# Who issues the first loads: the two context transfers move from SyncE's queue to ScalarE's, ahead of its table load

## The reference, cut to what matters

```python
def _L0_xattn_ref(q, latent_kv, Wq, Wkv_expand, Wout):
    qp = q @ Wq.T
    kv = latent_kv @ Wkv_expand.T          # context (.., 256) -> keys and values, 1024 each
    k, v = jnp.split(kv, 2, axis=-1)
    ...
    scores = jnp.einsum('bhqd,bhkd->bhqk', qh, kh) * inv_sqrt_d
    scores = jnp.where(causal, scores, jnp.finfo(scores.dtype).min)
    attn = jax.nn.softmax(scores, axis=-1)
    out = jnp.einsum('bhqk,bhkd->bhqd', attn, vh)
    return out @ Wout.T

x = x + _L0_xattn_ref(_layernorm(x, axis=-1), ctx_512, Wq, Wkv_expand, Wout)
x = x + _L0_attn_ref(_layernorm(x, axis=-1), ...)   # gated MLP with quantized weights
x = x + _L0_ffn_ref(_layernorm(x, axis=-1), ...)    # 8 routed experts and a shared one
```

## Time and profile before

| | us |
|---|---|
| median of 3 runs | 627.8 (627.37 to 627.97) |
| the profiled execution | 628.29 |
| its span, first to last instruction | 626.5 |
| PE busy | 609.5 (97% of the span) |
| DVE busy | 507.5 (81%) |
| ACT busy | 427.5 (68%) |
| POOL busy | 192.8 (31%) |
| bytes moved | 177.91 MB, mean 284 GB/s |

### The profile page before, as it was taken

One profiled execution on the slowest core, in us unless ns is written; L12 is line 12 of the kernel. 1 busy time (PEld: TensorE's weight loads), 2 busy tenths in 40 slices (PEclk: granted clock), 3 DMA queues, 4 the chain that ended last, 5 costly groups with the idle time before them and its releaser, 6 DMA issues.

```text
span 626.5 us, 10607 instructions
## 1 busy us (share of the span) xinstructions
PE 609.5 (97%) x3624; PEld 477.4 (76%) x3625; DVE 507.5 (81%) x883; ACT 427.5 (68%) x563; POOL 192.8 (31%) x174
## 2 busy tenths in 40 slices
PE   7999999998999999999999999999999999999995
PEld 6778888887887444444567888898998989889784
DVE  5888888888787787889899479788696887968687
ACT  3998888889755988888585366649385583846630
POOL 2254445425100243435940310040330404314051
PEclk9999999999999999999999999999999999999999
DMA  8977776865236997936999759695886968769357
GB/s 311 421 311 310 304 307 243 310 268 201 101 138 248 416 367 282 383 123 252 402 357 419 323 195 322 244 385 205 310 309 211 384 230 307 291 237 367 121 174 271
DMA packets 31070, 177.91 MB, mean 284 GB/s; under 512 B 4064, under 2 KB 4064, under 8 KB 14784
## 3 DMA queue, kind: packets, MB, share of 16 engines
q1 hardware_dynamic: 25536, 158.64, 66.0%
q0 software_dynamic: 5504, 18.88, 8.3%
HBM read 154.30 MB, written 23.20 MB: 283 GB/s over the span
## 4 chain that ended last, share of the span: by engine, by line
PE 69%; ACT 13%; DVE 7%; DMA 4%; issue 3%; POOL 2%; SPq 0%; DVEq 0%; POOLq 0%; ACTq 0%
PE BK L2215 11%; PE BK L307 9%; PE BK L1903 8%; PE BK L1946 6%; PE BK L2218 4%; ACT RA L1395 4%; ACT PR L1422 4%; PE BK L313 3%; PE BK L314 3%; PE BK L319 3%; PE BK L2185 3%; PE BK L2173 2%; PE BK L1848 2%; DVE WL L1038 2%; PE BK L2171 2%
## 5 line engine op out<-in xcount | busy, mean ns | idle before, releaser
L2215 PE MATMUL BK<-EX,WH 128*128 128x320 f32 x384 | 99.4, 343 | 0.0
L705 POOL TENSOR_TENSOR WL<-RC,WH 128x2048 fp32r<-128x2048 f32 x7 | 45.6, 6508 | 167.9 <-ACT WH L1603 167.9
L1038 DVE TENSOR_TENSOR WL<-RA,WH 128x2048 fp32r<-128x2048 f32 x40 | 89.3, 2288 | 9.2 <-ACT WH L1603 8.8
L2218 PE MATMUL BK<-EX,WL 128*128 128x160 f32 x336 | 79.3, 236 | 0.0
L1603 ACT ACTIVATE WH<-RA 128x2048 fp32r<-128x2048 f32 x40 | 73.7, 1908 | 0.8 <-PE BK L1946 0.8
L2215 PEld LDWEIGHTS BK<-EX,WH 128*128 128x128 f32 x384 | 69.2, 189 | 0.0
L2218 PEld LDWEIGHTS BK<-EX,WL 128*128 128x128 f32 x336 | 64.2, 191 | 0.0
L655 POOL TENSOR_TENSOR HB<-HB,ND (+2 forms) x26 | 28.6, 1120 | 100.5 <-DVE BH L922 99.8
L1712 ACT ACTIVATE HX<-SR 128x320 fp32r<-128x320 f32 x16 | 7.5, 472 | 57.0 <-DVE SR L1088 57.0
L1494 ACT ACTIVATE RA<-RA,RT 128x2048 int16<-128x2048 f32 x22 | 43.7, 1997 | 2.7 <-DVE RT L852 1.9
L1903 PE MATMUL BK<-TG,XQ 128*128 128x512 bf16 x192 | 42.4, 379 | 0.1
(11 more groups left out here) (336 smaller groups left out, 1660.9 us busy)
## 6 DMA issues: line engine op xcount, KB each, us to landing
RA<-wbit SPq DMA_DIRECT2D x54, 1024.0 KB, 6.4
RA<-wmoe SPq DMA_DIRECT2D x40, 1024.0 KB, 6.2
RC<-wmoe SPq DMA_DIRECT2D x20, 1024.0 KB, 7.8
rows<-ZERO POOLq DMA_DIRECT2D x40, 256.0 KB, 8.2
XG<-rows SPq DMA_DIRECT2D x10, 512.0 KB, 3.6
rows<-YS SPq DMA_DIRECT2D x9, 512.0 KB, 4.1
RA<-wqk SPq DMA_DIRECT2D x7, 640.0 KB, 8.1
RA<-wo SPq DMA_DIRECT2D x4, 1024.0 KB, 8.0
```

Of the source, the lines that this page charges most:

```text
L705: e.tensor_tensor(WL[2][:, at], RC[5][:, :], WH[2][:, at].bitcast(f32), ALU.subtract).then_inc(free_c[5], 1)
L1038: e.tensor_tensor(WL[m][:, q * RAW:q * RAW + RAW], RC[j][:, :], WH[m][:, q * RAW:q * RAW + RAW].bitcast(f32), ALU.subtract)\
L2215: mm = e.matmul(bank[GBK[f]][:, 0:2 * R], WH[m][:, at], EX[:, k, :, :].rearrange("p a b -> p (a b)"), start=k == 0, stop=k == KD - 1)
L2218: e.matmul(bank[GBK[f]][:, 0:R], WL[m][:, at], EX[:, k, 0, :], start=False, stop=False)
```

## The change

The two loads of the context leave SyncE's program and become the first two instructions of ScalarE's, ahead of its table load. They have the same source, target, size and semaphore as before. SyncE's program begins with the first weight block, and everything behind it stands in the same order as before. Nothing else is changed.

```diff
         @blk.sync
         def _(e):
-            e.dma_start(CTX[:, 0, :], ctxT[:, 0, :]).then_inc(s("ctx_in"), 16)
             e.dma_start(RA[0][:, 0:DM], wv[:, 0:DM]).then_inc(s("wv_in"), 16)
-            e.dma_start(CTX[:, 1, :], ctxT[:, 1, :]).then_inc(s("ctx_in2"), 16)
             for t in range(NT):
...
         @blk.scalar
         def _(e):
+            e.dma_start(CTX[:, 0, :], ctxT[:, 0, :]).then_inc(s("ctx_in"), 16)
+            e.dma_start(CTX[:, 1, :], ctxT[:, 1, :]).then_inc(s("ctx_in2"), 16)
             e.preload_act_table(ACT.Sqrt)
+
             def context_hi(m):
```

## The result

The changed kernel takes 628.89 us (median of 22 runs, 627.95 to 630.88) and the kernel before 627.77 (22 runs beside them, 627.00 to 628.86). The ratio is 1.0018, with a 95% interval of 1.0012 to 1.0025: slower by 1.1 us. Forecast were 627.6 and a range up to 628.6, so the prediction was wrong in its sign, and the time lies 0.3 us outside its range. The loss is within the 0.2% that the prediction took for the same, and it is clear of zero.

A forecast was written before the change was run, and what follows sets the result against it. TensorE was taken to set the opening's pace, the DMA engines being the second limit. Shortening two waits (0.17 us on TensorE, 0.16 on VectorE) was to start the exponentials 0.20 sooner: 627.8 - 0.20 = 627.6 us, range 627.0 to 628.6.

The forecast's parts named there:

- The bound of the kernel: Opening: TensorE sets the pace, the DMA engines are the second limit, busy all the time from 6 us on.
- SyncE's issues, d = 0.3: SyncE's queue: two issues fewer shift the whole stream of loads sooner by d, taken as 0.3 us, between -0.3 and 0.78.
- ScalarE's issues: Ahead of ScalarE's table load: two added issues of 0.45 us each, table load at 1.70, hidden in idle time, cost 0.
- Context 0 is issued at about 0.80 as before: no change beyond sharing (below): First context load, now on ScalarE's queue: issue time unchanged at about 0.80, no cost entered for its landing.
- Context 1, "lands sooner than 7.69", "gain 0": Second context load: issued at 1.25 for 1.73, lands sooner, but TensorE first needs it at 12.94, so gain 0.
- Rival A: Opening: sharing makes the first weight block land late, at 7.69 at worst, costing 1.09 us, 628.9 in all; chance 0.10.
- The first wait, 0.17 us on TensorE ... gain 0.17: TensorE's idle time before its first L307: gone if the second weight block lands at least 0.2 us earlier; gain 0.17.
- The second wait, 0.16 us on VectorE: VectorE's wait for the load before L764: L764 starts 0.30 us sooner, the first exponentials 0.20 sooner, at 35.18.
- B: Rival on the opening's loads: bound by bytes, d = 0, both waits stay, nothing moves, 627.8 us; chance 0.27.
- C: Rival on the opening's loads: two interleaved queues lose, d = -0.3, both waits grow by 0.3, 628.1 us; chance 0.11.
- D: Rival on later stages: shifted loads gain more than the opening's waits, put at 627.0 us; chance 0.07.
- From there on: After the first exponentials: head pairs follow at a fixed 16.04 us, so their gain carries to the end and nothing adds.

The follow-up runs named there:

- e2: Against the kernel before, only context block 0 moved to ScalarE's queue, SyncE's beginning with the first weight block; 628.49 us, ratio 1.0009 (0.9995 to 1.0023).
- e1: Against the kernel before, only context block 1 moved to ScalarE's queue, context 0 staying first in SyncE's; 628.37 us, ratio 1.0006 (0.9997 to 1.0014).
- e7: The changed kernel with the first weight block as two loads of 2 KB rows; 627.85 us, ratio 1.0003 (0.9994 to 1.0013) against the kernel before.

## Why the prediction was wrong

**The bound of the kernel** (the multiplies, with the load for L764 close behind): right. The floor is seen in four profiles.

**SyncE's issues, d = 0.3:** not decided. Against the profile that the prediction used, the second weight block was usable 0.47 us sooner, and the share from 3 to 6 us rose from 0.74 to 0.92. Against the second profile of the same kernel it was 0.60 later, and the share there was 0.90. The kernel by itself moves these by more than the change did; that 0.47 lies near 0.3 is luck. (By the earlier trace rows six loads and not five had been issued by 3.7.)

**ScalarE's issues:** right. 0.44 and 0.49 us apart, the table load at 1.73, hidden.

**"Context 0 is issued at about 0.80 as before: no change beyond sharing (below)":** this is the step that failed. Below stood the price of sharing for the weights and none for context 0. It lost 2.71 us. The prediction's own rows give its cover: ScalarE's further wait of 1.36 us behind the copy, and the 0.64 us by which the values' operands were ahead of TensorE, 2.00 in all. 2.71 - 2.00 = 0.71 had to show, and `values_first` started 0.66 later. What I should have asked of each load that stays at its place is who is served beside it now. At the head of the one queue context 0 was usable at 3.82 to 3.97, and the change took that place away.

**Context 1, "lands sooner than 7.69", "gain 0":** wrong too. It was usable at 8.68, for it stands behind context 0 in a queue that gets a third of the bytes. What needs it is not only the first L307 but VectorE, whose low half of it stands ahead of the statistics and of L747. In the profile after this was the load at the head of the chain. No run delays context 1 alone as far as that, so its share of the loss isn't shown apart; with context 0 alone moved (e2) the mark was 0.13 short of the whole, and there context 0 itself was 0.14 sooner.

**Rival A** had the mechanism, two queues served side by side, with the wrong victim: it was the small early load that came late, while the weights landed at 6.5, inside the 6.6 from which A would have counted. Its price of 1.09 and its time of 628.9 are met by luck. They were the worst case of a landing at 7.69, and the measured loss is made of 0.81 and 0.37 on VectorE. I gave A 0.10, because I measured its cover at the weights. By turns of one packet each, 256 KB in 2 KB rows beside 4 KB rows need 768 KB through the engines, and 768 KB had taken until 5.96. This estimate could have been worked out from the rows of before, and it would have shown context 0 1.99 us late, at the very end of its cover. The 0.7 us beyond it, from 5.96 to 6.68, the runs show (6.54 to 6.69 in four profiles) but don't take apart.

**"The first wait, 0.17 us on TensorE ... gain 0.17":** wrong in sign. The condition was met (a landing over 0.2 sooner than in that profile), and L747 still did not get ready sooner. VectorE came to it 0.81 late, from the context, and found GpSimd at work: 0.37 more after the change, 0.76 in e1. It took both. With the block 0.47 sooner GpSimd began at 12.30, and a VectorE free at 12.07, as before, would have been first. I had named what is late next on ScalarE and not looked at who else waits for the same load. The earlier trace rows hold VectorE's side only. GpSimd's row in the same profile, half a microsecond behind VectorE's start, would have shown how little kept them apart:

```profile
12.77 1.34 POOL L629 TENSOR_TENSOR WVL<-RA,WVH 128x512 fp32r<-128x512 f32 x1 [8.79 <-ACT WVH L1351]
```

**"The second wait, 0.16 us on VectorE":** it didn't come to it. SyncE issued the load for L764 at 25.04 and not at 23.88, because it waits for GpSimd's low halves, which were late as all the rest. It landed near 32.8, and VectorE came to it at 33.39 without a wait.

**Rivals B, C and D:** B and C both rest on the size of d, which isn't decided, and neither has the late context blocks that made the loss; D's gain elsewhere is not there, since the loss at the exponentials is the loss at the end. **From there on:** right, 1.10 at the exponentials and 1.08 at 147 us.

What the hold is made of is in part argued. The runs show that VectorE and GpSimd don't work on these subtractions side by side. Where GpSimd began first, VectorE ended 0.54 to 0.55 after GpSimd's recorded end, wherever it had begun (six profiles). Where VectorE began first, GpSimd ended 1.15 to 1.16 after VectorE's: 14.11 after 12.96 before the change, 13.24 after 12.08 in the second profile of it, 13.51 after 12.36 in e7. In all nine the second one needed its own length (0.69, 1.29) less 0.13 to 0.15, counted from the first one's end. That is what one would see if the second began its work some 0.14 us ahead of the first one's recorded end and not sooner. The Trainium skill (SBUF — State Buffer, "Who interferes with whom") says that a VectorE instruction with two inputs in the buffer and a GpSimd instruction that reads it exclude each other, and that the one that starts first keeps the shared ports for its whole length. By that rule, the rows agree on who loses in all nine. That it is these ports and not something else that the two share, and what the 0.14 us are, no run here shows.

## What to carry to other kernels

A load's place in a queue is a priority. Moving a small, urgent load to an empty queue of its own doesn't make it first but gives it turns with the large ones, and by packets: with half the row size it got a third of the bytes. Keep it first in the one queue, or give what flows beside it rows as short as its own; both kept this kernel level with before, and neither made it faster.

When a transfer moves, list everyone who waits for it. An engine off the path may start sooner than the one that is on it and get in its way.

Before a landing in one profile is set against a landing in another, profile the same kernel twice: here one load's landing moved by 1.07 us without any change.

## What the runs showed of the hardware

VectorE's subtraction of 128x512 (0.69 us alone) took 1.06 to 1.79 when GpSimd's of the same shape (1.29 us) was running at its start, and ended 0.54 to 0.55 after it in six profiles. Begun first, it took 0.69 in three profiles, and GpSimd's then took 1.34, 1.54 and 1.62 and ended 1.15 to 1.16 after it.

Two queues with rows of 4 KB and 2 KB sent 156 and 144 packets in 3 us, and 0.58 and 0.27 MB. With the first weight block's rows at 2 KB as well, it was 251 and 232 packets, and 0.51 and 0.43 MB.

The level of 2.4 GHz began between 6.11 and 9.18 us in twelve profiles whose TensorE started at 3.15 to 3.17 alike; in two profiles of one kernel, at 7.20 and 6.11.

Beside two issues by ScalarE (0.42 and 0.46 us) SyncE's first three took 0.39 and 0.89 for two, and without them 0.39 for the first and 0.91 for the same two.
